# Gated delta rule: the transposed blocks of the first merge level made by Pool and sent by way of DRAM, with other orders of work

## The reference

```
S = S * exp(g_t)
kv = einsum('bhk,bhkv->bhv', k_t, S)
delta = (v_t - kv) * b_t
S = S + k_t[..., :, None] * delta[..., None, :]
o = einsum('bhk,bhkv->bhv', q_t, S)
```

## Time and profile before

| | |
|---|---|
| median of 3 runs | 4582.89 us (4578.5 to 4586.45) |
| the profiled execution | 4581.29 us, its span 4579.3 us |
| busy, TensorE matmul / weight load | 3966.9 / 3077.2 us (87% / 67%) |
| busy, VectorE / ScalarE / Pool | 2462.0 / 1990.2 / 1085.3 us (54% / 43% / 24%) |
| mean granted TensorE clock | 0.924 |
| delta rule stage | from about 2070 to 4110 us of the span |

### The profile page before, as it was taken

How to read it: one execution, slowest core, us unless ns; L and a number is a source line. 1 busy time by engine, 2 the same in 40 slices (tenths; PEclk the granted TensorE clock), 3 DMA queues, 4 the chain that set the end, 5 groups by cost and what they waited for, 6 DMA issues and landing times. The chain is left out here.

```text
span 4579.3 us, 72621 instructions
## 1 busy us (share of the span) xinstructions
PE 3966.9 (87%) x23860; PEld 3077.2 (67%) x23860; DVE 2462.0 (54%) x5456; ACT 1990.2 (43%) x4069; POOL 1085.3 (24%) x1689
## 2 busy tenths in 40 slices
PE   5887788698999999993798888888888888769998
PEld 3555555377888888881576767676767677646666
DVE  7888888452222222224577777777777676421111
ACT  5655655111222222212466666666666566432222
POOL 0111111102222222212343333333333332200000
PEclk8888888799999999996799999999999999879999
DMA  1010010345555555552111111111111110011111
GB/s 34 29 42 28 28 42 20 75 135 179 183 183 183 184 183 185 183 170 68 39 42 40 43 41 42 42 42 38 42 43 42 42 42 25 20 51 55 55 55 46
DMA packets 220427, 345.91 MB, mean 76 GB/s; under 512 B 99956, under 2 KB 171380, under 8 KB 201972
## 3 DMA queue, kind: packets, MB, share of 16 engines
q1 hardware_dynamic: 196404, 271.69, 18.7%
q0 software_dynamic: 23760, 71.07, 4.9%
HBM read 275.56 MB, written 67.63 MB: 75 GB/s over the span
## 5 line engine op out<-in xcount | busy, mean ns | idle before, releaser
L525 ACT ACTIVATE moe_rel<-moe_fc 128x512 f32<-128x512 f32 x284 | 169.6, 597 | 798.5 <-PE moe_fc L490 798.5
L490 PE MATMUL moe_fc<-moe_xT,moe_win 128*128 128x256 f32 x2272 | 503.8, 380 | 1.5 <-issue 0.8
L501 PE MATMUL moe_o<-moe_wout,moe_hT 128*128 128x256 f32 x2272 | 502.0, 379 | 0.0
L490 PEld LDWEIGHTS moe_fc<-moe_xT,moe_win 128*128 128x128 f32 x2272 | 433.1, 191 | 60.8 <-issue 2.1
L501 PEld LDWEIGHTS moe_o<-moe_wout,moe_hT 128*128 128x128 f32 x2272 | 426.6, 190 | 54.8
L549 DVE TENSOR_TENSOR moe_hT<-moe_rel 128x512 f32<-128x512 f32 x284 | 196.7, 693 | 361.0 <-ACT moe_rel L525 361.0
L1776 DVE SCALAR_TENSOR_TENSOR gdr_y<-gdr_bank,gdr_cw,gdr_y 128x511 f32<-128x511 f32 (+2 forms) x384 | 287.5, 749 | 79.8 <-ACT gdr_y L2044 59.3
L2251 PE MATMUL gdr_bank<-gdr_hT,gdr_wqkv 128*128 128x512 f32 x512 | 261.7, 636 | 41.5 <-ACT gdr_qk L2059 24.6
L558 DVE COPY moe_osb<-moe_o 128x512 f32<-128x512 f32 x71 | 49.1, 692 | 424.9 <-PE moe_o L501 424.9
L723 DVE TENSOR_TENSOR ffn_z<-ffn_o,ffn_xres 128x512 f32<-128x512 f32 x32 | 20.6, 686 | 381.5 <-PE ffn_o L690 381.5
L679 PE MATMUL ffn_fc<-ffn_xT,ffn_win 128*128 128x512 f32 x512 | 224.5, 597 | 1.2 <-ACT ffn_xT L699 1.2
(11 more groups left out here) (391 smaller groups left out, 8584.6 us busy)
## 6 DMA issues: line engine op xcount, KB each, us to landing
moe_win<-in_moe_w SPq DMA_DIRECT2D x71, 1024.0 KB, 7.9
moe_wout<-in_moe_w SPq DMA_DIRECT2D x71, 1024.0 KB, 5.1
slots_out<-moe_osb POOLq DMA_DIRECT2D x71, 256.0 KB, 7.4
ffn_xin<-mixed_rows SPq DMA_DIRECT2D x17, 512.0 KB, 3.8
gla_xp<-in_xT_rows SPq DMA_DIRECT2D x16, 512.0 KB, 4.7
gla_xres<-in_x_rows SPq DMA_DIRECT2D x16, 512.0 KB, 3.9
token_rows<-gla_x POOLq DMA_DIRECT2D x16, 512.0 KB, 3.4
rt_W<-in_fc_b SPq DMA_DIRECT2D x32, 256.0 KB, 3.3
```

The costliest lines, as they stand in the source:

```text
L490: ins = nc.tensor.matmul(fc_ps[j][:, m % 2, :], win[u][:, c, m * P:(m + 1) * P], xT[:, c, :], start=(c == 0), stop=(c == DT - 1))
L501: ins = nc.tensor.matmul(o_ps[u][:, t, :], hT[u][:, k, t * P:(t + 1) * P], wout[u][:, k, :], start=(k == 0), stop=(k == FT - 1))
L525: nc.scalar.activation(rel[:, j, :, :], fc_ps[j][:], ACT.Relu).then_inc(relu_done, 1)
```

## The change

1. At level 4 TensorE no longer transposes T and ScalarE no longer copies it to U. Instead Pool turns the inverted blocks (`vturn`, one operation after `vblk`), SyncE stores them to a second DRAM tensor, and loads them onto the diagonal of U[2 * pair] and U[2 * pair + 1] in 16 small DMAs of four blocks each, behind the eight of T. `second_half` of level 4 waits for all 16 (`u_in`). `restart` clears U[t] as well as T.
2. At level 6, L2374 makes only the 64 rows that count (`rows_of`), and the copy to Y takes only these.
3. VectorE makes R of chunk 2 before `products` in slot 0, in the order that TensorE has.
4. Three output transposes and their copies come ahead of the transposes to tokens in slot 9 and one behind, in place of two and two.
5. `reach` and `rates(1)` move from slot 12 to slot 11, `reach` ahead of `mix_out(1)`.

```diff
@@ SyncE, return_blocks
                     sp.wait_ge(s["vmade"], b * 2 + pair + 1)
-                    sp.dma_start(blocks_in.rearrange("g k m i -> (g k) m i"), vblk[:]).then_inc(v_out, 16)
+                    sp.dma_start(blocks_in[0].rearrange("g k m i -> (g k) m i"), vblk[:]).then_inc(v_out, 16)
+                    sp.wait_ge(s["vturned"], b * 2 + pair + 1)
+                    sp.dma_start(blocks_in[1].rearrange("g k m i -> (g k) m i"), vturn[:]).then_inc(vt_out, 16)
                     sp.wait_ge(v_out, (b * 2 + pair + 1) * 16)
                     sp.wait_ge(s["rst"], b * TT + 2 * pair + 2)
                         for k in range(NB):
                             sp.dma_start(T[block(k), :, :, block(k)].rearrange("m a h i -> m (a h) i"),
-                                         blocks_in[:, k, :, :].rearrange("g m i -> m g i")).then_inc(t_in, 16)
+                                         blocks_in[0][:, k, :, :].rearrange("g m i -> m g i")).then_inc(t_in, 16)
+                        sp.wait_ge(vt_out, (b * 2 + pair + 1) * 16)
+                        for k in range(NB):
+                            for i in range(2):
+                                sp.dma_start(U[2 * pair + i][block(k), :, block(k)],
+                                             blocks_in[1][i * DH:(i + 1) * DH, k, :, :].rearrange("g m i -> m g i")).then_inc(u_in, 16)
@@ Pool, invert_blocks
-                    waiter(pool, b)[1]("vmade", pair + 1, ins)
+                    done = waiter(pool, b)[1]
+                    done("vmade", pair + 1, ins)
+                    done("vturned", pair + 1, step(vturn[:], vblk[:].rearrange("g m i -> g i m"), ones[0:GB, 0:SUB_].unsqueeze(1).broadcast_to([GB, SUB_, SUB_]), ALU.mult))
@@ VectorE, period
-                        if here and lv < 0:
-                            products(pair, b)
                         t, part = CHUNK_AT.get(slot, (None, None))
                         if t is not None and t >= 2 and past:
                             chunk(t, part, b - 1, w)
+                        if here and lv < 0:
+                            products(pair, b)
@@ ScalarE, restart and half_level
+                        a_op(U[t][:], id4[:], ACT.Copy, scale=0.0)
                         done("rst", t + 1, a_op(T[:, t % 2, :, :], id4[:], ACT.Copy, scale=0.0))
-                    wait("ut", n)
-                    done("U", n, copy(U[t][:], heads(bank[UT][:])))
+                    if lv > BASE:
+                        turned = turn_of(t, lv - BASE - 1, LEVELS - 1 - BASE)
+                        wait("ut", turned)
+                        done("U", turned, copy(U[t][:], heads(bank[UT][:])))
                     wait("y", n)
-                    done("Ye", n, copy(Y[i][:], bank[YZ[i]][:, 0:DH * HP].rearrange("p (h c) -> p h c", h=DH)))
+                    done("Ye", n, copy(Y[i][rows_of(lv), :, :], bank[YZ[i]][rows_of(lv), 0:DH * HP].rearrange("p (h c) -> p h c", h=DH)))
@@ ScalarE, period
                         if past and slot == 9:
-                            turned_o(0, b - 1)
-                            turned_o(1, b - 1)
+                            for c in range(DH - 1):
+                                turned_o(c, b - 1)
                         if front and 2 <= slot <= NP_ + 1:
                             spread_out(slot - 2, b + 1)
                         if past and slot == 9:
-                            turned_o(2, b - 1)
-                            turned_o(3, b - 1)
+                            turned_o(DH - 1, b - 1)
+                        if front and slot == 11:
+                            rates(1, b + 1, w)
                         if front and slot == 12:
-                            rates(1, b + 1, w)
@@ TensorE, first_half and second_half
-                    if i or lv > BASE:
-                        wait("U", turn_of(t, lv - BASE) - 1)
-                    for h in range(DH):
-                        ins = tp(bank[UT][:, h * P:(h + 1) * P], T[:, i, h, :], ident[:])
-                    mark("ut", ins)
+                    if lv > BASE:
+                        if i or lv > BASE + 1:
+                            wait("U", turn_of(t, lv - BASE - 1, LEVELS - 1 - BASE) - 1)
+                        for h in range(DH):
+                            ins = tp(bank[UT][:, h * P:(h + 1) * P], T[:, i, h, :], ident[:])
+                        mark("ut", ins)
-                        ins = mm(bank[YZ[i]][:, h * HP:(h + 1) * HP].rearrange("p (m n) -> p m n", n=half), nAT[:, i, h, :], first,
-                                 start=True, stop=True)
+                        ins = mm(bank[YZ[i]][rows_of(lv), h * HP:(h + 1) * HP].rearrange("p (m n) -> p m n", n=half),
+                                 nAT[:, i, h, rows_of(lv)], first, start=True, stop=True)
-                    wait("U", turn_of(t, lv - BASE))
+                    if lv > BASE:
+                        wait("U", turn_of(t, lv - BASE - 1, LEVELS - 1 - BASE))
+                    else:
+                        pe.wait_ge(u_in, (b * 2 + t // 2 + 1) * (2 * 16 * NB))
@@ TensorE, period (turn_o like turned_o above)
+                        if front and slot == 11:
+                            reach(b + 1)
                         if past and slot == 11:
                             mix_out(1, b - 1)
-                        if front and slot == 12:
-                            reach(b + 1)
```

More of the change, by code:

```diff
@@ L1443, in delta_rule @@
         NB, GB = P // SUB_, 2 * DH * P // SUB_
-        wblk, vblk, tblk, id16, low16 = (sb(n, [GB, SUB_, SUB_]) for n in ("wblk", "vblk", "tblk", "id16", "low16"))
+        wblk, vblk, tblk, vturn, id16, low16 = (sb(n, [GB, SUB_, SUB_]) for n in ("wblk", "vblk", "tblk", "vturn", "id16", "low16"))
         nAT, T = sb("nAT", [P, 2, DH, P]), sb("T", [P, 2, DH, P])
@@ L1484, in delta_rule @@
                    gp=TT, gt=TT, aB=TT, DT=TT, kk=TT, na=TT, qd=TT, kd=TT, gs=1, gx=1, gb=1, rst=TT,
-                   z=INV, T=MERGED, ut=INV, U=INV, y=INV, Ye=INV, Uf=TT, vmade=2, S=TT + 1, ks=TT, R=TT, qse=TT, dl=TT, de=TT, su=TT,
+                   z=INV, T=MERGED, ut=MERGED, U=MERGED, y=INV, Ye=INV, Uf=TT, vmade=2, vturned=2, S=TT + 1, ks=TT, R=TT, qse=TT, dl=TT, de=TT, su=TT,
                    op=TT, o=TT, osq=TT, ov=1, orr=1, og=DH, oT=DH, oTe=DH, en=2, xe=2, tl_var=2, tl_rstd=2, n2=1, xa=1, n2T=2,
@@ L1491, in delta_rule @@
         xn_stored, hT_stored, x2_in, hTg_in, x3_stored = (sem(n) for n in "xn_stored hT_stored x2_in hTg_in x3_stored".split())
-        n_out, w_blk, v_out, t_in, base_step = (sem(n) for n in "n_out w_blk v_out t_in base_step".split())
+        n_out, w_blk, v_out, vt_out, t_in, u_in, base_step = (sem(n) for n in "n_out w_blk v_out vt_out t_in u_in base_step".split())
         mix_step, ln_step, aff_step, cv_step, l2_step, soft_step, qk_step, gate_step, tail_step, last_step, res_step = (
@@ L1513, in delta_rule @@
         x_of = lambda t, u: XT0 if t < 2 else XT1[u]
+        rows_of = lambda lv: slice(0, P) if lv < LEVELS - 1 else slice(HP, P)
         v_of = lambda t, u: (v0 if t < 2 else v1[u])[:, t % 2, :, :]
@@ L2469, in period @@
                                 pe.wait_ge(s["qd"], b * TT + TT)
-                            turn_o(0, b - 1)
-                            turn_o(1, b - 1)
+                            for c in range(DH - 1):
+                                turn_o(c, b - 1)
                         if front and 2 <= slot <= NP_ + 1:
@@ L2485, in period @@
                         if past and slot == 9:
-                            turn_o(2, b - 1)
-                            turn_o(3, b - 1)
+                            turn_o(DH - 1, b - 1)
+                        if front and slot == 11:
+                            reach(b + 1)
                         if past and slot == 11:
                             mix_out(1, b - 1)
-                        if front and slot == 12:
-                            reach(b + 1)
                         if front and slot in (12, 13):
@@ L2526, in build_program @@
     blocks = (2 * DH, P // SUB_, SUB_, SUB_)
-    blocks_out, blocks_in = (nc.dram_tensor(name, blocks, F32).ap() for name in ("blocks_out", "blocks_in"))
+    blocks_out = nc.dram_tensor("blocks_out", blocks, F32).ap()
+    blocks_in = [nc.dram_tensor(name, blocks, F32).ap() for name in ("blocks_in", "blocks_turned")]
     slots_out = scratch("slots_out", SLOTS, D)
```

## The result

The changed kernel takes 4711.06 us (median; 4698.34 to 4721.13) where the kernel before takes 4584.67 beside it: the ratio is 1.0268, with a 95% interval of 1.0243 to 1.0293. It is slower, as forecast, but by 126 us where 63 were forecast, and ends 11 us above the range. The span grew by 117 us, from 4579.3 to 4696.7.

A forecast was written before the change was run, and what follows sets the result against it. The DRAM round trip to T's arrival, then TensorE's queue, bounds each half period. Fourteen periods at 2.4 + 2.0 = 4.4 give 62, the edges +1: 4581.3 + 63 = 4644, or 4646 as median; range 4560 to 4700.

The forecast's parts named there:

- U's arrival: SyncE's 16 loads at 0.47 us land U 7.5 us after T; L2386 of level 4 starts 2.9 and 1.5 later.
- rival A: SyncE's U loads are cheap, 0.23 us apart, so the kernel gets faster: 3.5 us less a period, 4534; chance 16%.
- The turn on Pool: One 64x256 Pool operation of 0.84 us with its store hides in T's wait for the first store; cost nothing.
- The output transposes: Three output transposes, then one, on TensorE: `mix_out` still waits for the fourth copy, so 0.
- The gain of 0 for `reach`: One slot earlier removes TensorE's 2.24 us `gam` wait, about 1.0 remaining for copies to XT; gain 0.
- What is given back after z4: After level 4's L2386, idle time and shorter level 6 work recover part of the delay, leaving +1.4 and +1.0 a period.
- Gain on the path 0: R first in slot 0 removes TensorE's 1.84 us wait, but TensorE then waits longer for T; gain 0.
- The clock: TensorE's idle waits before level 4's L2386 lower its clock on work behind: 1.0 us each pair, +2.0 a period.
- rival C: L2386 of level 4 is late and the clock falls further, 2.1 us after each of two waits: 4675; chance 20%.
- The round trip: From the products through DRAM to T's arrival: latency of 29.3 us in pair 0 and 31.5 in pair 1, unchanged.
- nAT isn't delayed, or by 0.1 us: VectorE in slot 0: R's 1.1 us fits in the 2.23 us idle before nAT, delaying it by at most 0.1.
- Edges: The first and last periods, where T is already waited for longer, add +1 us together.

The follow-up runs named there:

- the filler run: The changed kernel plus useless identity transposes on TensorE in each pair, 14 before the wait for T and 28 before that for U; ratio 1.0101 to the kernel before.
- half_rows_alone: The kernel before with only the half rows at level 6 (L2374 makes 64 rows); ratio 1.0001.
- r_first_alone: The kernel before with only R of chunk 2 made ahead of the products in slot 0; ratio 0.997.
- u_in_8_loads: The changed kernel with U of all four tiles in one tensor, so 8 loads of 128 runs replace 16 of 64; ratio 1.005 to the kernel before.
- the version with TensorE's transposes: The changed kernel with level 4's U made by TensorE again, output transposes two and two, 16 identity transposes before pair 0's wait for T; ratio 0.9937 to the kernel before.
- u8_turns: The changed kernel with U in 8 loads and the output transposes two and two again, without useless transposes; ratio 1.0023 to the kernel before.
- the filler before T: The changed kernel with U in 8 loads, output transposes two and two, and 16 identity transposes before pair 0's wait for T; ratio 0.9972 to the kernel before.

## Why the prediction was right or wrong

**U's arrival** was right. The pace of the new loads, which no row had shown, is 0.47 us in 17 of the 32 pairs (0.47 was taken) and up to 0.54 in the others; U lands 7.1 to 8.6 us after T (7.5), and T's arrival to z4 grew by 4.4 us a period, the forecast 2.9 + 1.5. The bound that the issue time doesn't follow what is moved held again with 8 loads of double size. With it rival A fell. The Trainium skill ("DMA: Bandwidth & Descriptors", section "Issuing engines are not separate DMA queues") says that the time to initiate a DMA is usually small beside the DMA itself; for these loads the trace disagrees, as issuing the 16 took 7.5 us and one lands 1.6 us after its issue.

**Costs put at nothing.** The turn on Pool (0.84 us, T's loads not pushed) and the later `hTg` and `x2`, for which no wait stands in the trace: right. The output transposes: right, 0. The gain of 0 for `reach` was right in its sum and wrong in its words. Of the 2.24 us for `gam` some 1.0 should have stayed as a wait for the copies to XT. The changed kernel's waits of TensorE in the 12 periods from 2423.8 to 3915.9 us (total us, times, longest) have

```profile
PE gdr_bank L2403 <- DMA gdr_U<-blocks_turned: 38.9, 21, 4.2
PE gdr_bank L2388 <- DMA gdr_T<-blocks_in: 33.9, 13, 3.4
PE gdr_bank L2299 <- ACT gdr_XT L2090: 29.0, 12, 2.4
```

that is 2.4 us for each wait for XT: it took the whole place of the wait for `gam`. The first line also says that the wait for U is met in 21 pairs of the 24, with 1.9 us each, not in all with 3 to 4: in the others TensorE's slower work fills it.

**What is given back after z4**, -2.0: right in its sum, as the filler run shows (-2.2), but by luck. It was put at -1.5 in pair 0 and -0.5 in pair 1; with both fillers it is -2.6 and +0.5. The half rows give nothing by themselves (`half_rows_alone`), and R first, which was put at 0 on the path, gives 0.3% (`r_first_alone`). There the step "Gain on the path 0" failed: the wait of TensorE for R did turn into a wait for T, but the forecast looked at TensorE alone up to T's arrival, and the gain lies behind z4.

**The clock** is the main term that was mis-sized, and the step of the forecast that failed. It was put at 1.0 us for each pair, 2.0 a period, from a row of pair 1 in period 5; the filler run gives 4.0 us a period behind z4 (46.9 - 42.9; 2.1 in pair 0 and 1.9 in pair 1) and 4.8 in the timed whole. The prediction took a row from T's arrival to z4, where the low clock is hidden by the wait for U, as price for the work behind z4. The price itself was read wrongly too. It is 5.7 less 4.7, and the 5.7 are 32 instructions of pair 1, the 4.7 are 44 of pair 0. 5.7 us at a clock of 0.60 hold 4.6 us at the lower level, and work that takes 4.6 us there takes 2.3 at the upper: a price of 2.3, not 1.0. Two windows of pair 1 from T's arrival to z4 in `u_in_8_loads`, one at each level, say the same for nearly equal work:

```profile
2504.45:2508.40 3.95, 3.12 (x28) 2.88 (x26) 1.45 (x5) 3.54 (x12) 0.00 (x0) 1.00 0.15 17
2742.91:2748.53 5.62, 5.62 (x29) 5.62 (x27) 1.50 (x5) 3.59 (x12) 0.00 (x0) 0.50 0.11 12
```

A better row would have been one of TensorE-bound work: in pair 1 of period 7 above, 27.1 us at 0.87 for 24.3 at 1.00. The rival C (2.1 us for each wait, 4675) was the nearest case.

**The round trip** was put at no change, and grew by 1.5 us a period. Some 1.0 of it lies before `nAT` is done and 0.9 between that and the landing of `wblk`; behind it 0.4 is made up. One part is the order of R and the products, of which the prediction says "nAT isn't delayed, or by 0.1 us": in `r_first_alone` `nAT` of pair 0 is done 0.6 us later after the products of TensorE than in `half_rows_alone` of the same set, and T lands 0.7 later. The rest stays open. Runs with a clock that stays up have part of the growth too (61.2 a period with both fillers), so the clock isn't all.

**Edges.** The first and last periods were put at +1 together. Periods 0, 14 and 15 and the pieces around them took 17 us of the 117: period 0 4.7, period 14 7.3, and 8.3 in period 15 and behind it, less 3.1 ahead of the stage. Why period 15 and what follows grew that much isn't shown.

So of the 54 us missed in the span (117 less 63), 23 lie behind z4 (13 periods of 1.8: the clock costs 2.0 more than forecast, the giving back 0.2 more), 20 in the round trip (13 of 1.5), and 11 in the edges (17, where the sum had 1 and 4.4 for period 14).

**What stays open**: why U in 8 loads, which lands before z4 needs it, is no faster than U made by TensorE. Its stretch behind z4 has 3.9 us a period at the low clock in pair 1 even with the filler, and the version with TensorE's transposes has none; whether the smaller amount of TensorE work between T and z4 brings that about, or the idle pieces ahead of it, no run separates. In `u_in_8_loads` and `u8_turns` TensorE also waits ahead of level 6's product in pair 1, 20.9 and 17.4 us in 13 periods where the changed kernel has 3.7; with the filler before T it is 3.7 again, so that isn't what is left. `reach` and `rates(1)` one slot earlier never ran alone.

## What to carry to other kernels

Where a round trip through DRAM bounds a stage, cost each small DMA at the queue's pace, not at its bytes, and ask which operand arrives last: 16 of them behind the one that was just in time took 7.5 us, and made z4 4.4 us a period later, to save 2 us of TensorE work. A wait that TensorE didn't have before is to be priced twice, as the wait and as the slower clock on the bound work behind it; filling it with useless transposes shows the second price in one run. The price at the lower level is half the time spent there, so compare equal work, and not two stretches with different work in them. And work taken off TensorE ahead of the last arrival bought nothing here, while an earlier start of R, priced at nothing, was worth 0.3%: follow such a step beyond the next wait.

## What the runs showed of the hardware

In period 7 an idle piece of 2.6 us ahead of T was followed by TensorE work at half speed: 7.4 us at a granted clock of 0.54, close to 0.5, the lower of its two levels (1.2 of 2.4 GHz); 14 to 16 transposes of the identity in such a piece kept the granted clock at 1.00, and made the kernel 0.5% faster (1.0023 to 0.9972) or, with 28 more before U in each pair of the changed kernel, 1.6% faster. SyncE's loads of U follow each other every 0.47 us in just over half of the pairs (up to 0.54 in the others) whether they move 4 KB (16 loads in 7.48 us) or 8 KB (8 in 3.74). ScalarE's copy to Y takes 367 ns in the mean for 64 partitions by 256 elements and 372 for 128 by 256. On Pool one 64x256 operation takes 0.84 us mostly; the eight slowest L1670 of the kernel before, up to 1.90 us, all lie beside a 2.29 us TENSOR_TENSOR of 128x2048 on VectorE.
